# Last group of experts in a decoder layer: where the output products of the last two groups stand, and how their halves are signalled

## What is computed

```python
xe = jnp.zeros((E, cap + 1, D), x.dtype).at[experts, pos_safe].set(xf[tokens])[:, :cap]
h = jax.nn.silu(jnp.einsum('ecd,edf->ecf', xe, W1)) * jnp.einsum('ecd,edf->ecf', xe, W3)
ye = jnp.einsum('ecf,efd->ecd', h, W2)
yp = ye[experts, jnp.minimum(pos_safe, cap - 1)]
out = jnp.zeros((T, D), x.dtype).at[tokens].add(wk[:, None] * yp)
```

## Time and profile before

| | us |
|---|---|
| median of 3 runs (1401.38 to 1402.80) | 1402.24 |
| the profiled execution, its own time | 1403.52 |
| its span, first to last instruction | 1401.8 |
| TensorE busy in the span | 1295.8 |
| VectorE busy | 930.0 |
| ScalarE busy | 640.0 |
| POOL busy | 418.9 |
| mean granted TensorE clock, share of full | 0.971 |

### The profile page before, as it was taken

The page is one execution under the profiler, slowest core; times in us unless marked ns, Lnnn a source line. Parts: engine busy times, 40 slices in busy tenths (PEclk is TensorE's granted clock), DMA queues, the critical chain, the costliest instruction groups (busy, mean ns, idle before and its releaser), DMA issues. The chain is left out here.

```text
span 1401.8 us, 33422 instructions
## 1 busy us (share of the span) xinstructions
PE 1295.8 (92%) x11085; PEld 1151.1 (82%) x11085; DVE 930.0 (66%) x2770; ACT 640.0 (46%) x1628; POOL 418.9 (30%) x741
## 2 busy tenths in 40 slices
PE   7799999999999999997579999999999999999995
PEld 5477777777777777776379999999999999999995
DVE  4578888888888888887546465565645656565541
ACT  2355555555545555554344344443534435344331
POOL 4114344433444344433402122222221212221222
PEclk9999999999999999998579999999999999999997
DMA  3831220101001010100042242533424234252221
GB/s 94 245 89 34 80 71 25 34 26 34 29 30 34 26 34 25 34 23 24 31 128 32 31 121 32 124 38 66 91 36 117 32 91 66 31 121 32 31 25 22
DMA packets 152459, 80.20 MB, mean 57 GB/s; under 512 B 106210, under 2 KB 145859, under 8 KB 152290
## 3 DMA queue, kind: packets, MB, share of 16 engines
q1 hardware_dynamic: 137698, 59.11, 16.8%
q0 software_dynamic: 14592, 18.91, 8.0%
HBM read 44.04 MB, written 33.96 MB: 56 GB/s over the span
## 5 line engine op out<-in xcount | busy, mean ns | idle before, releaser
L903 ACT ACTIVATE h_a<-banks 128x256 f32<-128x256 f32 x320 | 122.3, 382 | 342.2 <-PE banks L1370 328.5
L1313 DVE TENSOR_TENSOR h_f<-banks,h_a 128x256 f32<-128x256 f32 x320 | 135.7, 424 | 144.3 <-ACT h_a L903 120.2
L520 POOL TENSOR_TENSOR idle_g<-half 128x1 f32<-128x1 f32 x144 | 32.2, 224 | 535.1 <-DVE y_s L1332 386.5
L1370 PE MATMUL banks<-xe_t_hi,w_even_hi 128*128 128x256 f32 x640 | 180.8, 282 | 3.3 <-issue 1.8
L1370 PE MATMUL banks<-xe_t_hi,w_even_lo 128*128 128x256 f32 x640 | 180.6, 282 | 1.1 <-issue 1.1
L1370 PE MATMUL banks<-xe_t_lo,w_even_hi 128*128 128x256 f32 x640 | 180.5, 282 | 0.0
L1370 PE MATMUL banks<-xe_t_hi,w_odd_hi 128*128 128x256 f32 x640 | 178.0, 278 | 0.0
L1370 PE MATMUL banks<-xe_t_lo,w_odd_hi 128*128 128x256 f32 x640 | 178.0, 278 | 0.0
L1370 PE MATMUL banks<-xe_t_hi,w_odd_lo 128*128 128x256 f32 x640 | 178.0, 278 | 0.0
L892 ACT ACTIVATE h_t_hi<-h_f 128x256 fp32r<-128x256 f32 x320 | 131.7, 411 | 32.6 <-DVE h_f L1313 31.9
L1320 DVE TENSOR_TENSOR h_t_lo<-h_f,h_t_hi 128x256 fp32r<-128x256 f32 x320 | 133.6, 418 | 6.1 <-ACT h_t_hi L892 4.4
(11 more groups left out here) (242 smaller groups left out, 3393.6 us busy)
## 6 DMA issues: line engine op xcount, KB each, us to landing
raw<-in_w SPq DMA_DIRECT2D x24, 1024.0 KB, 8.1
expert_rows<-empty SPq DMA_DIRECT2D x4, 2580.0 KB, 11.4
x_blocks<-expert_rows SPq DMA_DIRECT2D x312, 32.0 KB
xin<-in_x SPq DMA_DIRECT2D x32, 128.0 KB, 2.2
out_dram<-x SPq DMA_DIRECT2D x32, 128.0 KB, 1.7
out_dram<-y_s,token POOLq DMA_INDIRECT x80, 4.0
mask_i<-in_mask SPq DMA_DIRECT2D x32, 32.0 KB, 1.9
expert_rows<-r_xn,send POOLq DMA_INDIRECT x64, 2.7
```

Source lines behind the costliest of these rows:

```text
L520: return pool.tensor_tensor(idle_g[:, i:i + 1], half[:, 0:1], half[:, 0:1], ALU.add)
L903: act.activation(h_a[:, f % 2, :], bank[2 + f % 4][:, 0:GS], ACT.Silu).then_inc(silu_ok, 1)
L1313: dve.tensor_tensor(h_f[:, f % 2, :], bank[2 + f % 4][:, GS:2 * GS], h_a[:, f % 2, :], ALU.mult)\
L1370: last = pe.matmul(dst, lhs, rhs, start=(i == 0), stop=(i == len(pairs) - 1))
```

## The change

Four things change, all for the last group (39) and the output of group 38.

1. On TensorE the tiles of group 39 are split: tiles 0 to 3, then the output product of group 38, then tiles 4 to 7. After them comes `last_results`, the output product of group 39.
2. `last_results` on TensorE writes its first half into bank 7 and its second into bank 1 (a bank of the chunk stage, unused by then), and raises `dn_mm` after each half.
3. On VectorE the reading out of group 38 moves in front of tile 4 of group 39. The copies of the row numbers of group 39 stand ahead of the wait for its product; each half is then scaled as soon as its own `dn_mm` is there, and raises `y_ok` by itself.
4. POOL waits for `y_ok` of the first half before the first DMA of group 39, and for `y_ok` of the second half before the second.

```diff
+        last_rows = [bank[7][:, 0:D], bank[1][:, 0:D]]
...
             def add_rows(g, par):
                 pool.wait_ge(y_ok, g + 1)
                 for a in range(2):
+                    if a and is_last(g, NG - 1):
+                        pool.wait_ge(y_ok, NG + 1)
...
+            def last_results():
+
+                dve.wait_ge(added, (NG - 2) * 32)
+                dve.wait_ge(about_landed[1], (NG - 2) * 8 + 16)
+                for a in range(2):
+                    dve.tensor_copy(token[1][a][:, :], about[:, 1, a, 0:1])
+                for a in range(2):
+                    dve.wait_ge(dn_mm, NG + a)
+                    dve.tensor_scalar(y_s[:, 1, a, :], last_rows[a], about[:, 1, a, 1:2], None, ALU.mult).then_inc(y_ok, 1)
+
...
                 for f in range(FT):
+                    if f == FT // 2 and is_last(g, NG - 1):
+                        results(g - 1, 1 - par)
                     gated(g, par, f)
...
-                if later(g, 1):
+                if later(g, 1) and not is_last(g, NG - 1):
                     results(g - 1, 1 - par)
...
-            results(NG - 1, 1)
+            last_results()
...
+            def last_results():
+
+                par, w = (NG - 1) % 2, w_s[1][2]
+                pe.wait_ge(h_lo_ok, NG * FT)
+                pe.wait_ge(y_ok, NG - 2)
+                for a in range(2):
+                    split_product(last_rows[a], [
+                        ([h_t[part][:, par, f, a * P:(a + 1) * P] for part in range(2)],
+                         [w[part][:, f // 4, (f % 4) * D:(f % 4 + 1) * D] for part in range(2)]) for f in range(FT)])\
+                        .then_inc(dn_mm, 1)
...
+                if is_last(g, NG - 1):
+                    hidden(g, j, range(FT // 2))
+                    results(d, j - 1)
+                    hidden(g, j, range(FT // 2, FT))
+                    return
                 hidden(g, j)
...
-            results(E // 2 - 1, GPL - 1)
+            last_results()
```

More of the change, by code:

```diff
@@ L1661, in split_product, with hidden @@
                 return product(dst, [(lhs[i], rhs[k]) for lhs, rhs in pairs for i, k in ((0, 0), (0, 1), (1, 0))])
-            def hidden(g, j):
+            def hidden(g, j, tiles=range(FT)):
                 par, w = j % 2, w_s[j // GPE]
                 pe.wait_ge(xet_ok, g + 1)
-                for f in range(FT):
+                for f in tiles:
                     n = g * FT + f
```

## The result

The changed kernel takes 1398.22 us in the median of 7 runs (1394.91 to 1399.6), against 1402.80 of the kernel before in 7 runs. The ratio is 0.9965, with a 95% interval from 0.9953 to 0.9978: 4.9 us faster, between 3.1 and 6.6. The forecast was 1398.5 us and a gain of 3.7. Run again beside the experiments it came to 0.998 (0.9968 to 0.9992), a gain of 2.8 us. Both intervals hold 3.7.

What follows compares the result with a forecast made beforehand. The end was set by when TensorE is through and how many DMA links lie behind it. The chain's -4.36 plus 0.7 for the clock gave -3.7 us: 1402.24 to 1398.5 us, range 1397.0 to 1400.4.

Steps and rivals of the forecast that it cites:

- The chain: POOL's accumulating DMAs at the end: group 39's first DMA no longer stands behind group 38's; last issue 1389.03 instead of 1393.39.
- the link: From one DMA issue on POOL to the `idle_g` its landing releases: taken as 3.85 us; the second half hides in it.
- the sum: Shift of POOL's last DMA issue from 1393.39 to 1389.03: -4.36 us, before any fall of the clock.
- The stall: TensorE before the last product, waiting for tile 7's low part: 2.22 us between matmul starts instead of 0.11, 2.1 new.
- The boundaries that were costed at nothing: TensorE at group 38's moved output and at tiles 4 to 7: no wait, at most 1.1 us if the readout's cover were gone.
- The clock: TensorE's clock may fall behind the stall: 1.4 us where it does, half of executions paying, 0.7 us in the median.
- The row at 22 us: Earlier trace row: clock fell at about 22.35 after TensorE was busy 1.6 of 3 us, so no long idle time needed.
- case B: TensorE's clock falls in nearly all executions: -4.36 + 1.4 to 1.6 us, 1399.3 to 1399.5; chance 0.26.
- A: TensorE's clock stays up in nearly all executions: -4.36 us, 1397.9; chance 0.36.
- C: Low clock lasts to the end of TensorE's last product: -0.9 us, 1401.3; chance 0.05.
- D: VectorE's first scaling starts only when both halves' products are done, despite separate signals: -1.6 us, 1400.6; chance 0.04.
- E: Slower DMA links for group 39's two landings: 4.8 us slower than before, 1407.0; chance 0.03.

Runs made afterwards that it cites:

- e3: The whole change, but the first half of the last output product waits for low parts one tile at a time (eight waits); 0.9965 of the kernel before.

## Why the prediction was right

**The chain.** Right in each step. The first DMA of group 39 is released by its rows, the second by a landing, the second half hides in the link with 1.5 us to spare (1.5 forecast), and group 38 has landed before its place is needed. Before and after are 30.50 and 27.02 us from mark to last issue, a gain of 3.48 between two profiles whose clock stayed up, against the -4.36 of the sum. Behind the last issue 8.42 us remain, 8.41 before.

**The 0.9 us between.** Two terms were sized too small. The first is TensorE's pace: I took 0.113 us for every matmul from the last groups of one trace. Tiles 0 to 3 of group 39, the product of group 38 and the last product ran at 0.118 in the changed kernel's profile: 0.41 us more up to group 38's scaling (11.31 against 10.90) and 0.11 in the first half of the last product. (The stall was 0.11 shorter than forecast and the step behind it, 1380.19 to 1380.42, 0.11 longer than the others, so these two cancel.) The trace before had it in plain sight, in the groups that came by turns. The second is the step from `idle_g` to the last issue, 0.65 us where I took 0.34; the kernel before shows both values in the earlier trace rows, and I took the commoner. Together 0.83 of 0.88. The pace is no doing of the change, though: against the estimate for before at the same pace the gain is 4.3, which is nearer to the sum than 3.48.

**The stall.** Its place, its releaser and its size (2.11 against 2.22 from start to start) are as forecast, and e3 shows that TensorE no longer waits when the waits go by tile. The boundaries that were costed at nothing cost nothing: the profile of the change has no other wait of TensorE in the last 46 us.

**The clock.** The size of the term was right: a fall costs 1.39 us where I took 1.4, and it comes in some executions and not in others (two of three profiles). That half of them pay was a guess, and three profiles don't confirm it. Were all to pay, the same sum gives 1399.3 us, still within the range, so that the median came out within 0.3 us of 1398.5 is in part luck. The Trainium skill's page "TensorE: Matmul & The Clock Gate" warns, in "Why this matters for your kernels", of longer gaps only; here 1.84 us of idle time were followed by a fall in two profiles. The row at 22 us pointed the right way, but the trace of the kernel before has a nearer one that the prediction didn't use, ahead of the tiles of group 20: an idle time of 1.79 us between dense 256-column matmuls.

```profile
1039.00:1040.00 1.00, 1.00 (x11) 0.97 (x9) 0.00 (x0) 0.00 (x0) 0.00 (x0) 1.00 0.06 16
...
1041.95 0.38 PE L1370 MATMUL banks<-xe_t_hi,w_even_hi 128*128 128x256 f32 x1 [1.79 <-issue]
...
1042.00:1043.00 1.00, 1.00 (x8) 1.00 (x9) 0.00 (x0) 0.00 (x0) 0.72 (x1) 0.97 0.21 18
1043.00:1044.00 1.00, 0.86 (x5) 0.57 (x3) 0.00 (x0) 0.00 (x0) 0.83 (x1) 0.50 0.23 26
```

The clock fell 1.0 us after the work had resumed. All nine profiles have this stall (1.79 to 2.44 us idle), and in all nine the clock fell at it; in one, 0.1 us before the work resumed. With the three stalls of 1.84 us at the end that makes 11 falls in 12, so case B deserved a larger share than A.

**The rivals.** C, low to the end, did not occur with this stall; the clock rose again inside the product each time. D is out: the first scaling ran while TensorE wrote the other bank. E: the links were 3.88 us. Whether 3.7 us or something nearer to 4.4 or 2.8 is the change's true median, the two measurements (4.9 and 2.8) leave open.

## What to carry to other kernels

Where a chain of DMAs ends a program, ask of each edit what the head of the chain waits for: an earlier result is worth nothing while an older transfer stands in front, and moving the older one is worth little while the last rows come in one piece. When work is moved that had covered a latency, count both the stall and what the stall may do to the clock of the work behind it; waits that go by tile remove both. And take the pace of an engine from several groups, not only from the last one.

## What was not expected

The two paces of 256-column matmuls at full clock, 0.1134 and 0.118 us, which change over where tiles follow an output product and can be changed by one further matmul ahead of the product (17.08 us a group with 256 columns, 16.66 with 16). And the step from `idle_g` to the issue of an indirect DMA, which is 0.34 or 0.65 us in the same program. And the stall ahead of group 20, which every profile has, of the kernel before too: the step from the scaling of group 18 to that of 19 takes 20.5 to 23.0 us where the others take 16.1 to 17.2, so that some 4 to 6 us are lost there, about as much as the change gains or more. What TensorE waits for is open; the trace names no releaser.
